# Delta rule on one core: TensorE's step regrouped by array tile size, the inverse spread over two steps

## What is computed

```python
u = attn @ v
w = attn @ k_beta
def step(S, inp):
    q_i, k_i, u_i, w_i = inp
    attn_i = jnp.where(lower_incl, q_i @ jnp.swapaxes(k_i, -1, -2), 0.0)
    u_adj = u_i - w_i @ S
    o_i = q_i @ S + attn_i @ u_adj
    S = S + jnp.swapaxes(k_i, -1, -2) @ u_adj
    return (S, o_i)
```

## Time and profile before

| | us |
|---|---|
| median of 3 runs (1385.19 to 1388.02) | 1387.27 |
| the profiled execution, its own time | 1384.97 |
| its span, first to last instruction | 1383.3 |
| TensorE busy in the span | 1255.4 (91%) |
| VectorE / ScalarE / GpSimd busy | 822.9 / 463.1 / 501.1 |
| mean granted TensorE clock (1.0 is the upper level) | 0.925 |

### The profile page before, as it was taken

How to read it: one execution, slowest core, us unless ns; L and a number is a source line. 1 busy time by engine, 2 the same in 40 slices (tenths; PEclk the granted TensorE clock), 3 DMA queues, 4 the chain that set the end, 5 groups by cost and what they waited for, 6 DMA issues and landing times. The chain is left out here.

```text
span 1383.3 us, 35769 instructions
## 1 busy us (share of the span) xinstructions
PE 1255.4 (91%) x12725; PEld 926.9 (67%) x12726; DVE 822.9 (59%) x1882; ACT 463.1 (33%) x1093; POOL 501.1 (36%) x711
## 2 busy tenths in 40 slices
PE   7999999989999999955989988298999999989998
PEld 5888888866777777733444445276888888856666
DVE  5778878725222222217999999368566666535553
ACT  1121111132222222214877878012222222213332
POOL 4344666513521111126666635223343444310000
PEclk9999999979999999987899988559899999969999
DMA  9999900012321111112354544912543333200001
GB/s 313 371 356 383 346 31 33 32 43 81 127 77 61 61 61 61 61 54 64 115 137 120 140 146 110 211 51 77 89 113 96 95 99 99 91 1 22 29 31 42
DMA packets 220107, 156.62 MB, mean 113 GB/s; under 512 B 111888, under 2 KB 201488, under 8 KB 219984
## 3 DMA queue, kind: packets, MB, share of 16 engines
q1 hardware_dynamic: 210672, 129.51, 31.6%
q0 software_dynamic: 9312, 25.44, 5.4%
HBM read 64.47 MB, written 90.44 MB: 112 GB/s over the span
## 5 line engine op out<-in xcount | busy, mean ns | idle before, releaser
L945 PE MATMUL ps_sc<-w,a_qeo 128*128 x568 | 183.3, 466 | 0.0
L753 DVE TENSOR_TENSOR a_stm<-a_vpad,ps_sc 128x352 f32<-128x352 f32 x71 | 37.0, 521 | 177.6 <-ACT a_vpad L517 161.7
L945 PEld LDWEIGHTS ps_sc<-w,a_qeo 128*128 128x128 f32 x568 | 104.1, 193 | 46.4 <-issue 2.3
L423 POOL DMA_DIRECT2D x_slots<-a_stm x66 | 36.3, 550 | 226.2 <-issue 226.2
L1596 PE MATMUL d_pp<-d_xT,d_w_p 128*128 128x512 f32 x192 | 109.0, 701 | 5.5 <-ACT d_xT L1332 5.5
L1492 DVE SCALAR_TENSOR_TENSOR d_cout<-d_cin,d_taps,d_cout 128x512 f32<-128x512 f32 x144 | 107.1, 754 | 3.8 <-ACT d_cout L1350 0.4
L915 PE MATMUL ps_kv<-w,a_stm 128*128 x426 | 105.9, 385 | 1.2 <-DVE a_stm L746 1.1
L915 PEld LDWEIGHTS ps_kv<-w,a_stm 128*128 128x128 f32 x426 | 79.4, 190 | 30.1 <-issue 12.5
L2381 PE MATMUL g_pp<-g_xT,g_w_g 128*128 128x512 f32 x192 | 89.3, 602 | 0.7 <-ACT g_xT L2233 0.7
L1262 POOL DMA_INDIRECT got<-x_slots,d_idx x64 | 74.4, 1163 | 18.8 <-issue 16.3
L517 ACT ACTIVATE a_vpad<-ps_sc 128x352 f32<-128x352 f32 x71 | 33.0, 464 | 140.3 <-PE ps_sc L945 140.3
(11 more groups left out here) (278 smaller groups left out, 2798.3 us busy)
## 6 DMA issues: line engine op xcount, KB each, us to landing
x_slots<-a_zeros SPq DMA_DIRECT2D x32, 1024.0 KB, 10.1
rec<-d_kve SPq DMA_DIRECT2D x32, 384.0 KB, 3.4
u_kve<-rec SPq DMA_DIRECT2D x32, 384.0 KB, 3.6
a_qeo<-x_slots SPq DMA_DIRECT2D x71, 128.0 KB, 2.0
x_slots<-a_stm POOLq DMA_DIRECT2D x66, 128.0 KB
rec<-d_act_out SPq DMA_DIRECT2D x32, 256.0 KB
u_qkT<-rec SPq DMA_DIRECT2D x32, 256.0 KB, 3.2
w<-in_w SPq DMA_DIRECT2D x4, 1408.0 KB, 14.2
```

What stands on the lines that cost most here:

```text
L753: dve.tensor_tensor(e_h[:, q, 0:HID], e_gate[:, q, :], ps_3[q], ALU.mult).then_inc(h_out, 1)
L945: mm = pe.matmul(ps, e_xT[:, q, k, :], w13[:, s, k, bass.ds(e_hidden, 1), :], start=(k == 0), stop=(k == KD - 1))
```

## The change

TensorE's step is put in another order: the 128x128 products first to last (q S, transposes, update of S, q k u, then k S and the output product of the next step), and between them five groups of small tiles: 64x64, 32x32, 64x64, 32x32, 64x64. The first part of the inverse moves from tile i-2 to i-1 (A), the second part stays at i-2 under a new name (M), the output product moves to tile i-5. The gram products are cut into tiles of 64x64: `gram(e, n)` makes 64 rows of k k and q k in one product of 256 columns and the other 64 in one of 128; the corner that the causal mask drops is zeroed once by a memset. Two `gram` calls stand around each of the products for u (L2055, L2090). The product with L2 goes into free columns of `b_y`, and the last one of the inverse into `b_1`. ScalarE copies both halves of u instead of VectorE. VectorE's `share` and `o2` move to the next step's start, the product into XT behind the normalisation; GpSimd makes L1 for tile i-1 at the start of its step and the scaled v one step later. A core of the diff:

```diff
+                a, asl, aq = i - 1, (k - 1) % 4, (k - 1) % 2
+                if has(a, NT):
+                    wait_apart(pool, loaded, rec_in[asl], 16 * (a - asl) + 64)
+                    wait_apart(pool, loaded, a1_done, a)
+                    pool.tensor_tensor(L1[:, :, :], l32[:, asl], low16[:, :].unsqueeze(1).broadcast_to([P, H, B32]),
+                                       ALU.mult).then_inc(l1_done, 1)
+
+                m, ms_, mq = i - 2, (k - 2) % 4, k % 2
+                if has(m, NT):
+                    length = small[:, bass.ds(m, 1), 4 * H:5 * H].rearrange("p a h -> p (a h)").unsqueeze(2).broadcast_to([P, H, DH])
+                    wait_apart(pool, loaded, less2_done, m - 1)
+                    pool.tensor_tensor(heads(vs[:, mq]), heads(kve[:, ms_, 1, :]), length, ALU.mult).then_inc(vs_done, 1)
...
-                t, s = i - 1, (k - 1) % 4
-                if has(t, NT):
-                    length = small[:, bass.ds(t, 1), 4 * H:5 * H].rearrange("p a h -> p (a h)").unsqueeze(2).broadcast_to([P, H, DH])
-                    wait_apart(pool, loaded, rec_in[s], 16 * (t - s) + 64)
-                    wait_apart(pool, loaded, less2_done, t - 1)
-                    pool.tensor_tensor(heads(vs[:, (k - 1) % 2]), heads(kve[:, s, 1, :]), length, ALU.mult).then_inc(vs_done, 1)
-                    wait_apart(pool, loaded, a1_done, t)
-                    pool.tensor_tensor(L1[:, :, :], l32[:, s], low16[:, :].unsqueeze(1).broadcast_to([P, H, B32]),
-                                       ALU.mult).then_inc(l1_done, 1)
...
+                if B:
+                    act.wait_ge(low_done, b + 1)
+                    wait(act, o_done, b)
+                    act.activation(u[0:64, :], b_2[0:64, 256:512], ACT.Copy).then_inc(low_out, 1)
...
+                if M:
+                    act.wait_ge(a2_done, m + 1)
+                    wait(act, p2_done, m)
+                    for e in range(2):
+                        rows = slice(64 * e, 64 * e + 32)
+                        z = act.activation(A2[rows], heads(b_y[rows, 256:384]), ACT.Copy)
+                    z.then_inc(a2_out, 1)
+                if B:
+                    act.wait_ge(u_done, b + 1)
+                    act.activation(u[64:128, :], b_2[64:128, 256:512], ACT.Copy).then_inc(u_out, 1)
...
-                    act.activation(GU[:, gs].rearrange("p (n e) c -> p e n c", e=2), b_g[0:64, :, 0, :, 64:128],
+                    act.activation(GU[:, gs].rearrange("p (n e) c -> p e n c", e=2), b_g[0:64, :, 1, :, 64:128],
...
+            dve.memset(b_g.rearrange("p e z n t -> p (e z n) t")[64:P, :, 0:64], 0.0).then_inc(g_zeroed, 1)
...
+                if C:
+                    dve.wait_ge(o_done, c + 1)
+                    wait(dve, o2_done, c)
+                    dve.tensor_tensor(heads(share[:, :]), heads(b_o[:, 0:D]),
+                                      per_head(c, 3), ALU.mult).then_inc(share_done, 1)
...
-                    dve.tensor_copy(u[low, :], b_2[low, 256:512]).then_inc(low_out, 1)
...
-                    dve.tensor_copy(u[high, :], b_2[high, 256:512]).then_inc(u_out, 1)
...
+                if M:
+                    dve.wait_ge(p2_done, m + 1)
+                    dve.wait_ge(xt_spread, m + 1)
+                    for e in range(2):
+                        rows = slice(64 * e, 64 * e + 32)
+                        z = dve.tensor_tensor(XT[rows, mq, :, 32:64], heads(b_1[rows, 0:128]), per_head(m, 0, rows, B32), ALU.mult)
+                    z.then_inc(p2_out, 1)
...
+                def gram(e, n):
+
+
+                    rows = slice(64 * e, 64 * e + 64)
+                    pe.matmul(b_g[low, e, :, n, :], qkT[rows, gs, 2 + n, low], qkT[rows, gs, n::2, :], start=True, stop=True)
+                    return pe.matmul(b_g[high, e, :, n, high], qkT[rows, gs, 2 + n, high], qkT[rows, gs, n::2, high],
+                                     start=True, stop=True)
...
+                if has(d, NT):
+                    pe.wait_ge(ot_out, d + 1)
+                    for n in range(KD):
+                        mm = pe.matmul(b_y[:, 0:D], oT[:, n, :], w_o[:, n, :], start=(n == 0), stop=(n == KD - 1))
+                    mm.then_inc(y_done, 1)
+                if G:
+                    wait_apart(pe, scaled, rec_in[gs], 16 * (g - gs) + 64)
+                    wait_apart(pe, scaled, stm_done, g)
+                    gram(1, 0)
...
                     wait_apart(pe, scaled, less_done, b + 1)
                     wait_apart(pe, scaled, p2_out, b + 1)
                     for h in range(H):
                         mm = pe.matmul(b_2[low, 256 + h * DH:256 + (h + 1) * DH], XT[low, bq, h, :], less[low, col(h, DH)],
                                        start=True, stop=True)
                     mm.then_inc(low_done, 1)
+                if G:
+                    gram(1, 1)
+                if A:
+                    wait_apart(pe, scaled, l1_done, a + 1)
+                    wait_apart(pe, scaled, x32_out, a)
+                    wait_apart(pe, scaled, p2_out, a - 1)
+                    for h in range(H):
+                        for r4 in range(4):
+                            rows = slice(32 * r4, 32 * r4 + 32)
+                            mm = pe.matmul(b_1[rows, col(h, B32)], L1[rows, h, :], x0[rows, asl, h, 1, :], start=True, stop=True)
+                    mm.then_inc(a1_done, 1)
+                if M:
+                    wait_apart(pe, scaled, x32_out, m + 1)
+                    wait_apart(pe, scaled, l_done, m + 1)
+                    wait(pe, y_out, i - 4)
+                    for h in range(H):
+                        for e in range(2):
+                            rows = slice(64 * e + 32, 64 * e + 64)
+                            mm = pe.matmul(b_y[64 * e:64 * e + 32, 256 + h * B32:256 + (h + 1) * B32], L2[rows, mq, h, :], XT32[rows, h, :],
+                                           start=True, stop=True)
+                    mm.then_inc(a2_done, 1)
+                if B:
+                    wait_apart(pe, scaled, gu_done, b + 1)
+                    wait_apart(pe, scaled, low_out, b + 1)
+                    for h in range(H):
+                        mm = pe.matmul(b_ku[high, col(h, DH)], GU[:, bs, h, :], u[low, col(h, DH)], start=False, stop=True,
+                                       skip_group_check=True)
+                    mm.then_inc(rest_of_ks, 1)
                 if A:
                     wait_apart(pe, scaled, a1_out, a + 1)
                     for h in range(H):
...
+                if M:
+                    wait_apart(pe, scaled, a2_out, m + 1)
                     for h in range(H):
-                        mm = pe.matmul(b_ku[high, col(h, DH)], GU[:, bs, h, :], u[low, col(h, DH)], start=False, stop=True,
-                                       skip_group_check=True)
-                    mm.then_inc(rest_of_ks, 1)
+                        for e in range(2):
+                            rows = slice(64 * e, 64 * e + 32)
+                            mm = pe.matmul(b_1[rows, h * B32:(h + 1) * B32], X32[rows, h, :], A2[rows, h, :], start=True, stop=True)
+                    mm.then_inc(p2_done, 1)
                 if G:
-                    wait(pe, rec_in[gs], 16 * (g - gs) + 64)
-                    wait(pe, stm_done, g)
-                    wait(pe, gu_done, g)
-                    for n in range(2):
-                        for z, what in enumerate((2, 0)):
-                            for e in range(2):
-                                rows = slice(64 * e, 64 * e + 64)
...
+                    gram(0, 0)
...
+                if G:
+                    gram(0, 1).then_inc(g_done, 1)
+                if B:
+                    wait(pe, share_done, b)
+                    for n in range(2):
+                        pe.matmul(b_o[:, col(n, P)], qkT[:, bs, n, :], S[:, 1 - bq, n, :], start=(n == 0), stop=False,
+                                  skip_group_check=True)
...
-                    wait(pe, y_out, c)
+                    wait(pe, y_out, i - 4)
```

105 lines of the change are left out of this document (24 added, 81 removed).

## The result

The changed kernel takes 1375.29 us (median of four runs, 1368.2 to 1377.26) against 1387.64 for the kernel before on the same chip (1385.19 to 1388.57): ratio 0.9912, 95% interval 0.9887 to 0.9936. That is a gain of 12.3 us, where 30.1 were forecast.

What follows compares the result with a forecast made beforehand. TensorE was taken as the bound, a step being as long as its groups. Savings of 24.8 + 0 + 3.6 + 1.2 + 0.5 = 30.1 from 1384.97 gave 1354.9, plus 2.3 for the median: 1357.2 us, range 1345 to 1380.

Steps and rivals of the forecast that it cites:

- Steps (1) to (4): TensorE's steady step: groups and tile-size changes sum to 7.68 us, taken as 7.8 with 0.1 added, against 9.04 before.
- (2): 64x64 gram tiles beside the products for u: overlapping, a group costs 0.86 us, which saves 0.12 us a step.
- (1): Grouping small tiles: twelve changes of tile size in a step become six, 1.85 us becomes 0.85, saving 1.00.
- (3): TensorE's idle 0.24 us a step, waiting for the copy of u, goes: ScalarE copies under other TensorE work.
- Rival (a): Matmuls start strictly in order, short products queueing behind wide ones: 8.4 us a step, gain 15, 1372 us; chance 0.18.
- Step (5): Steps 13 to 33: twenty steps at 7.8 instead of 9.04 us, saving 24.8 us.
- Rival (b): TensorE's clock falls where it now idles, above all steps 9 to 12: costs 14.5 us, 1372 us; chance 0.10.
- Step (6): Steps 9 to 12: sends on the DMA queue hold the loads, 37.0 us before and after, no gain.
- Step (7): Steps 3 to 8: 3.6 us saved in the first two at the lower clock, 1.2 in steps 5 to 8.
- Step (8): Start and tail: A and its copies come one step earlier, 37 steps remain; 0.5 us saved.

Runs made afterwards that it cites:

- the loop from step 5: The aligned kernel with gram groups first in its first three steps, TensorE's loop over steps 5 to 32, and 37 waiting instructions instead of 120: 1345.05 us, ratio 0.9704.
- the aligned kernel: The changed kernel with TensorE's loop begun at step 8 instead of 16 and 120 waiting instructions ahead of its first step: 1361.14 us, ratio 0.9847.
- the early loop: TensorE's loop begun at step 8 instead of 16: changed kernel 1444.21 us, ratio 1.0411; kernel before 1385.08 us, ratio 0.9994.

## Why the prediction was wrong

- **Steps (1) to (4), the step**: right. 7.8 us was forecast, 7.81 measured. The small groups of L2104, L2108 and L2115 take 0.97, as the sum has them (0.60 + 0.25 + a change of 0.12); a gram group takes 1.01 against 0.86 + 0.14, so short and long products do overlap as (2) took it. The wide group costs 0.31 a step more where (2) says 0.12, but it also needs a change of tile size of its own, 0.19 in (1): 0.31 together. (3) says 0.24 for the idle time and puts it down to ScalarE's copy; the idle time did go, but VectorE's copy has the same cover.
- **Rival (a)**, strict order in the array, falls: its group of about 1.3 us is 1.01. The Trainium skill, "TensorE: Matmul & The Clock Gate", section "The mechanism", by which it would hold, isn't borne out for float32 products on different tiles. In the rows above the second pass of the wide product starts at 1107.75, behind narrow ones (1107.49) and ones for u (1107.50) that stand after it in the program, and the group takes 1.01 us. That they also end while a wide one runs can't be said, since the ends are modelled.
- **Step (5), steps 13 to 33**: this is where it failed. 24.8 us became 5.3. "I followed all engines through a step and each result was ready" asks of TensorE only that its data be there; that its instructions be there was taken for granted, as the kernel before, with as many packets and no gap, seems to allow: the wait that was missing from the path is the one for the next 256 instructions. It cost 9.3 us of gaps and, with the clock, 10.1 more. With the fetches moved out of the stretch, the same steps give 21.0 of the 24.8, and 24.4 with the loop from step 5 (156.5 us).
- **Rival (b)**, the clock, came in, but by another road: not through idle time in steps 9 to 12 but behind the gaps. Its price was of the right kind, 14.5 for 34 us at the lower level, 0.43 for each; here 10.1 for 21 in steps 13 to 33, 0.48 for each. The prediction's own sign of being wrong, a granted clock of 0.50 beyond step 13, is there.
- **Step (6), steps 9 to 13**: 37.0 forecast, 39.7 measured. The sends do delay a load here: u_kve of tile 11, issued at 1004.73 between two groups of sends, lands 4.3 us later. GpSimd waits 5.5 us for it, and TensorE 1.70:

```profile
1009.05 0.43 PE L2044 MATMUL u_bank_g<-u_qkT 64*64 64x256 f32 x1 [1.70 <-DMA u_kve<-rec]
```

  The lower clock follows from 1010.38 on. The other gaps, 0.4 to 0.8 us, again begin a new 256. But the sends don't hold the stretch at 37.0. The kernel with the loop from step 5 has the same sends in it, no idle time, and takes 31.25 us, 4 x 7.81: that is the 31.2 which (6) held to be out of reach. So 5.8 us were given away by an argument from the DMA queue alone. Why its loads come in time and those of the changed and the aligned kernel don't wasn't tested.
- **Step (7)**: 4.8 forecast, 5.8 measured. TensorE's wait behind the inverse rows stands where it was said to go, at the first 64x64 group; its row in the waits of steps 0 to 31 is

```profile
PE u_bank L2068 <- DVE u_less L1963: 8.3, 4, 4.2
```

  As it had lower-clock stretches of its own, the agreement is partly luck.
- **Step (8), start and tail**: the start isn't 0 but costs 4.9 from first product to step 3, since the order that is right in the steady step puts the inverse between the halves of the gram tile when there is nothing else to do. The tail gained 6.2, most of it in step 33: 10.88 us at 0.76 in the kernel before, 6.53 at 1.00 here. The 5.2 us at the lower level there are some 2.2 of the 4.4 (an estimate, at 0.43 for each); the rest is work that step 33 no longer has, since the first part of the inverse is done a step earlier.
- The sign held. 1375.29 lies in the stated 1345 to 1380, but only because that range had the rivals in it; the forecast's own was 1347 to 1366. The sum was wrong by the two terms that it took as given, instruction supply and start.

The proof that the forecast gain was there: the kernel with the loop from step 5 is 40.0 us shorter in its trace than the kernel before (1343.3 against 1383.3). Of these, 31.1 are in steps 3 to 33, for which the prediction had 29.6. What it shows is the steady step: 24.4 of the 24.8 in steps 13 to 33. That the sums agree is luck, for in steps 9 to 13 it gains 5.8 where 0 was forecast, and in steps 3 to 9 only 0.9 where 4.8 was.

## What to carry over

A sum of durations says what an order of products can reach, not that the engine's instructions arrive in time: when a change packs many short instructions together, look for the packets of the instruction queue in the trace of before, and ask what the code costs that runs only once. A loop that is held by the engine is worth beginning as early as its register values allow. When a kernel's time moves with the place of its code, compare stretches of the trace from one event to the next: the same edit, the early loop, made the changed kernel 69 us slower, 14 us faster with 120 waits ahead of it, and left the kernel before as it was.

## What was not expected of the hardware

- **Instruction packets can stop TensorE.** Gaps of 0.8 to 2.6 us, ending 2.2 to 2.9 us after a 16 KB packet begins, each at the start of a new 256 instructions. The Trainium skill, "Runtime: NRT & Kernel Launch", section "Instruction fetch mechanics", says that the next page is fetched while the current one runs, so that crossing a block is mostly hidden; the kernel before bears that out (ten packets in 78 us, no gap), the changed one doesn't (eleven packets, five gaps). It also says that a taken branch to code outside the current window costs a fetch, and that unrolled code is preferred for it. The stops of 2.4 to 2.9 us behind the jump back in the loop that is fetched again agree; the jumps of the other loops, with no packet and no stop, show code of 6.4 packets that is kept. And the loop was the faster form here, by the 6.3 us above.
- **The place of a loop decides whether it is fetched again.** The same loop of 1627 records a turn: no packet from one place, 17 in 95 us from another, 1361 against 1444 us. By what rule is open.
- **A stop of about 2 us can lower the clock for 3.4 to 10.2 us**, and did behind five of eight; stops of 0.72 and 1.33 us didn't in eight cases.
- **Waiting instructions aren't free**: in the trace of the aligned kernel they start 0.108 us apart, 13 us for the 120 on a semaphore long set. They run while the loads are under way and outlast them: TensorE's wait at the start of the stage is 29.3 to 29.8 us with 120 or more, 23.9 with 67, and 20.7 to 22.7 with 37 or none.
- **Long and short products on different array tiles overlap**: 1.01 us, change of size included, for a group that in turn would take 1.79 without it, by the prediction's sum.
